# Recommendation tower on one core: ids counted from a partition's first row for two halves, and eight tables read by one-hot columns in the first half in place of seven

## The reference

```
e = jnp.stack([tbl_0[ids[:, 0]], ..., tbl_26[ids[:, 26]]], axis=1)   # 2048 x 27 x 128
dot = jnp.einsum('bnd,bmd->bnm', e, e)                               # pairs i < j are kept: 351
h = jnp.concatenate([z, dense_ctx], axis=1)                          # 367
h = jnp.maximum(h @ W_top1 + b_top1, 0.0)                            # 512
h = jnp.maximum(h @ W_top2 + b_top2, 0.0)                            # 256
y = h @ W_top3
```

## Time and profile before

| | |
|---|---|
| median of 3 runs | 383.13 us (382.71 to 384.81) |
| profiled execution, its own time | 381.17 us |
| its span (first to last instruction) | 379.3 us |
| PE busy | 345.7 us, 91% |
| DVE busy | 294.4 us, 78% |
| POOL busy | 269.3 us, 71% |
| ACT busy | 153.3 us, 40% |
| mean granted TensorE clock | 0.987 of full speed |

### The profile page before, as it was taken

The page is one execution under the profiler, slowest core; times in us unless marked ns, Lnnn a source line. Parts: engine busy times, 40 slices in busy tenths (PEclk is TensorE's granted clock), DMA queues, the critical chain, the costliest instruction groups (busy, mean ns, idle before and its releaser), DMA issues.

```text
span 379.3 us, 9954 instructions
## 1 busy us (share of the span) xinstructions
PE 345.7 (91%) x4035; PEld 322.6 (85%) x4035; DVE 294.4 (78%) x821; ACT 153.3 (40%) x217; POOL 269.3 (71%) x287
## 2 busy tenths in 40 slices
PE   1788868599999999999999999999999999999985
PEld 1677767588999999998999999998999999998874
DVE  4986696898688969798689969798689869793432
ACT  3352644434343453534343453534243453533421
POOL 6777877777777777777777777777777777777400
PEclk9989996999999999999999999999999999999999
DMA  6995225953333333334333333333343343221100
GB/s 184 251 247 136 64 63 137 213 186 96 82 93 85 79 84 82 95 69 95 82 94 85 79 86 81 95 72 91 85 91 85 76 89 83 76 57 50 36 2 1
DMA packets 22988, 36.38 MB, mean 96 GB/s; under 512 B 6224, under 2 KB 17120, under 8 KB 22944
## 3 DMA queue, kind: packets, MB, share of 16 engines
q0 software_dynamic: 8896, 18.24, 20.2%
q1 hardware_dynamic: 14048, 17.52, 18.6%
HBM read 35.73 MB, written 0.01 MB: 94 GB/s over the span
## 4 chain that ended last, share of the span: by engine, by line
PE 75%; POOL 14%; issue 5%; DMA 3%; ACT 2%; DVE 1%; ACTq 0%; DVEq 0%
PE embT_ps L410 35%; PE gram_ps L442 13%; POOL emb L379 12%; PE h_ps L470 11%; PE h_ps L494 7%; PE embT_ps L420 6%; DMA emb<-in_tbl,idx 3%; PE flat_ps L453 2%; POOL flatT L379 2%; ACT embT L634 1%; DVE flat L568 1%; DMA idx<-in_idx_rows 0%; PE h_ps L481 0%; PE flat_ps L481 0%; DVE flat L569 0%
## 5 line engine op out<-in xcount | busy, mean ns | idle before, releaser
L379 POOL DMA_INDIRECT emb<-in_tbl,idx x272 | 261.8, 962 | 83.8 <-issue 80.6
L537 DVE TENSOR_SCALAR one_hot<-ids,row_of 125x256 fp32r<-125x256 int32 x658 | 205.4, 383 | 13.2 <-PE embT_ps L410 10.6
L410 PE MATMUL embT_ps<-one_hot,tbl 125*128 125x256 f32 x1284 | 182.0, 297 | 13.0 <-DVE one_hot L537 11.4
L410 PEld LDWEIGHTS embT_ps<-one_hot,tbl 125*128 125x128 f32 x1284 | 166.7, 196 | 17.9 <-issue 8.9
L634 ACT COPY embT<-embT_ps 128x256 f32<-128x256 f32 x77 | 48.0, 624 | 134.2 <-PE embT_ps L410 129.0
L642 ACT COPY embT<-embT_ps 128x512 f32<-128x512 f32 (+1 forms) x80 | 80.7, 1012 | 11.7 <-PE embT_ps L420 11.7
L568 DVE STREAM_TRANSPOSE flat<-gram_ps 128x864 f32<-128x864 f32 x31 | 33.5, 1082 | 43.7 <-PE gram_ps L442 43.1
L442 PEld LDWEIGHTS gram_ps<-embT 128*59 128x59 f32 x1984 | 56.2, 134 | 9.6 <-ACT embT L634 3.9
L442 PE MATMUL gram_ps<-embT 128*59 128x54 f32 x1984 | 60.2, 217 | 3.8 <-ACT embT L634 2.3
L420 PE MATMUL embT_ps<-ident,emb 128*128 128x128 f32 x272 | 43.8, 276 | 11.6 <-DMA emb<-in_tbl,idx 8.6
L420 PEld LDWEIGHTS embT_ps<-ident,emb 128*128 128x128 f32 x272 | 32.2, 142 | 13.8 <-DMA emb<-in_tbl,idx 11.4
(11 more groups left out here) (47 smaller groups left out, 85.0 us busy)
## 6 DMA issues: line engine op xcount, KB each, us to landing
ids<-in_ids_hot SPq DMA_DIRECT2D x77, 128.0 KB
emb<-in_tbl,idx POOLq DMA_INDIRECT x272, 3.1
embT<-in_tbl SPq DMA_DIRECT2D x5, 448.0 KB
w_sb<-in_tbl SPq DMA_DIRECT2D x3, 560.0 KB
w_sb<-in_W_ring SPq DMA_DIRECT2D x1, 756.0 KB
w_sb<-in_W_top SPq DMA_DIRECT2D x1, 512.0 KB
h1T<-in_tbl SPq DMA_DIRECT2D x1, 448.0 KB
w_sb<-in_tbl SPq DMA_DIRECT2D x1, 448.0 KB
```

What stands on the lines that cost most here:

```text
L379: pool.indirect_dma_start(gathered_row(t, s), None, tables[f][:, :], bass.IndirectOffsetOnAxis(ap=idx[:, t, f:f + 1], axis=0),).then_inc(g ...
L410: mm = pe.matmul(out[:, 0:HN], tbl[0:ROWS, part, AT[o] + chunk, :], one_hot[0:ROWS, k % SLOTS, c, :], start=(chunk == 0 and part == 0), st ...
L537: done = dve.tensor_scalar(one_hot[0:ROWS, k % SLOTS, c, :], of, row_of[0:ROWS, KINDS.index(CH[o]), chunk:chunk + 1], None, ALU.is_equal)
```

## The change

Two things are edited. `READ_IN_HALF[0]` goes from 7 to 8: table number 7 is read by one-hot columns in half 0 as well, and tiles 0 and 1 gather 19 tables each. And for the builds of halves 0 and 1 (`RELATIVE` = 8 + 10 = 18 steps) ACT first turns the ids in their buffer into floats, the number of the partition's first row minus the id; DVE then compares that float with the constant -c for chunk c, in place of an int32 with a column of `row_of`. Builds from half 2 on are as before. In the start SP loads the ids of step 0 ahead of table 0 instead of behind it.

```diff
-READ_IN_HALF = (7, 10, 10, 10, 10, 10, 10, 10)
+READ_IN_HALF = (8, 10, 10, 10, 10, 10, 10, 10)
@@
+    RELATIVE = len(HOT0) + len(hots_of(1))
@@ SP
+            load_ids(0)
             for o in range(SHARED + 1):
                 load_table(o)
-                if o < len(HOT0):
+                if 0 < o < len(HOT0):
                     load_ids(o)
@@ DVE, build(n)
-                dve.wait_ge(ids_loaded[n % IDS], 16 * (n // IDS + 1))
+                if n < RELATIVE:
+                    dve.wait_ge(ids_relative, n + 1)
+                else:
+                    dve.wait_ge(ids_loaded[n % IDS], 16 * (n // IDS + 1))
...
+                        if n < RELATIVE:
+                            done = dve.tensor_scalar(columns, of.bitcast(F32), float(-chunk), None, ALU.is_equal)
+                        else:
+                            done = dve.tensor_scalar(columns, of, row_of[0:ROWS, KINDS.index(CH[o]), chunk:chunk + 1],
+                                                     None, ALU.is_equal)
@@ ACT
+            def relative_ids(n):
+                act.wait_ge(ids_loaded[n % IDS], 16 * (n // IDS + 1))
+                if n == 0:
+                    act.wait_ge(rows_ready, len(KINDS))
+                kind = KINDS.index(CH[HOTS[n][2]])
+                act.activation(ids[0:ROWS, n % IDS, :].bitcast(F32), ids[0:ROWS, n % IDS, :], ACT.Identity,
+                               bias=row_of[0:ROWS, kind, 0:1], scale=-1.0).then_inc(ids_relative, 1)
@@
             AHEAD = 3
+            relative_ids(0)
             for o in range(AHEAD):
                 split_high(o)
+                if o > 0:
+                    relative_ids(o)
@@ in the loop over ORDER, ahead of the copy of a hot step
+                    if n + AHEAD < RELATIVE:
+                        relative_ids(n + AHEAD)
```

More of the change, by code:

```diff
@@ L281, in dlrm_tower @@
         low_ready = sem("low_ready")
+        ids_relative = sem("ids_relative")
         ids_loaded = [sem(f"ids_loaded{b}") for b in range(IDS)]
@@ L536, in build @@
                         chunk = i * GROUP + c
-                        done = dve.tensor_scalar(one_hot[0:ROWS, k % SLOTS, c, :], of,
-                                                 row_of[0:ROWS, KINDS.index(CH[o]), chunk:chunk + 1], None,
-                                                 ALU.is_equal)
+                        columns = one_hot[0:ROWS, k % SLOTS, c, :]
+                        if n < RELATIVE:
[3 more added lines that the diff above has]
+                                                     None, ALU.is_equal)
                     done.then_inc(hot_built, 1)
```

## The result

| | before | after |
|---|---|---|
| median | 383.02 us (380.39 to 384.81, 9 runs) | 386.69 us (386.04 to 389.67, 9 runs) |
| profiled execution | 381.17 | 386.81 |
| span | 379.3 | 385.0 |
| ratio | | 1.0126, 95% interval 1.0091 to 1.0161 |

The change made the kernel slower by 1.3%. I had forecast no change that a measurement can tell (-0.6 us), so the sign was wrong. The number is almost that of my first rival (386.9), but not its mechanism, as the profile and the experiments show.

A forecast was written before the change was run, and what follows sets the result against it. POOL's gathers up to PE's last wait at 81.35 were taken to bind, then fixed PE work. -2.5 (two gathers) + 2.2 (contention) - 0.3 (small losses) = -0.6 us: profiled 380.6, median 382.5, range 379.5 to 387.5.

The forecast's parts named there:

- first rival: Gathers lose the shared pair to whole groups of new builds, 6.6 us; 386.9 us, chance 0.27.
- The step that failed: ACT's wait for ids n+3 ahead of copy n, in half 1: requested when build n-1 is done; taken as 0.
- The cover: PE's 11.0 us of idle time from 38 to 82 us, taken to hide delays there.
- The two gathers: Two fewer gathers, in tiles 0 and 1, ahead of PE's last wait: 2.5 us less on the bounding chain.
- The eighth table's 4.2 us of PE work: Half 0: net 4.2 us more PE work ahead of 39 us, covered by 14.3 us idle; taken 0.
- 0.9 us later: Tile 0 would end 0.9 us later, less a transpose, from the new order of tables between quads; taken 0.
- The new build: DVE builds, halves 0 and 1: 0.17 us each at double rate against 0.314, saving 21 us less 1.7, off the chain.
- the reason I gave against the Trainium skill's rule: Old build's 0.314 us means its operand column or int32 holds it at the single rate, despite the rule.
- The gathers beside new builds: 54 gathers on POOL wait for double-rate builds holding the shared pair: 2.2 us more, between 0 and 6.6.
- 0.3 of small losses: Small gather losses beside old builds, 3 ahead of 82 us, would go: 0.3 us less.
- PE's last wait: Sign of a wrong forecast: before PE's full stretch, this wait is for ACT or one_hot instead of a gather.
- The sum without the failed step: Whole-kernel forecast of -0.6 us, in which the wait for ids counted 0; forecast's chance 0.38.

The follow-up runs named there:

- f1: Kernel after, with the loads of tables 8 and 9 and layer 1's weights two places later in SP's queue, behind ids; 382.66 us, 1.0018 to before.
- f4: f3, with ScalarE waiting for the ids where the conversions stood, converting nothing; 389.98 us, 1.0228 to the kernel before.
- f3: Kernel before with only READ_IN_HALF[0] = 8: eight tables, old builds, no conversions; 380.85 us, 0.9974 to the kernel before.
- f2: Kernel after with READ_IN_HALF[0] back to 7, keeping new builds and conversions; 385.83 us, 1.0102 to the kernel before.
- g1: Kernel after with conversions and new builds for the first 13 steps in place of 18; 381.24 us, 0.9993 to the kernel before.
- g3: f1 with ids kept int32, compared with a constant; one run, 381.02 us, only record lengths read (306 ns on average).
- g4: f1 with float ids compared with an operand column in SBUF; one run, 379.89 us, only record lengths read (385 ns on average).

## Why the prediction was wrong, point by point

- **The step that failed** is the one on ScalarE's wait: "In half 1 the ids for n+3 are asked for when build n-1 is done. Taken: 0." The semaphore was right, the queue was left out. The request for ids n+3 stands in SP's queue behind loads that wait for something else, and twice these are tables 8 and 9, which wait for splits. Before, nobody needed these ids until later: only VectorE waited for them, at its own build 13. The change put the wait three steps earlier, on the engine that also empties PE's banks and starts the splits. In numbers: 0 was taken; the kernel after against f1 says 1.1% of 383, 4 us, and f4 against f3 says 2.5%, some 9 us without the new builds.
- **The cover.** I had 11.0 us of PE's idle time from 38 to 82 us as cover for anything of ScalarE's. It was used: pauses of 9.49 and 8.91 us on ScalarE became 4.22 and 3.41 us on PE, in place of waits for gathers, and the reads behind them ran at half clock, 1.6 us longer each than at full clock (3.78 against 2.14). The kernel before had slow reads as well (3.04 and 3.45 us), so against it the same steps took only about 1.9 us more work, and against f1 about 4.0. That a pause costs clock on top of its own length was not in the sum.
- **The two gathers** (-2.5): right for the gathers. f3 has the 54th gather 2.5 us earlier than the 56th was. How much of it reaches the end is smaller, -1.0 us with an interval from -2.1 to +0.1 (0.9974).
- **The eighth table's 4.2 us of PE work** at no cost: right by f2 and f3. But tile 0 did not end 0.9 us later: tile 1's first quad, at 38.01 before, is at 39.86 in f3, and at 41.40 in the kernel after and 41.41 in f2. So the 3.4 us are there without the table too, with the new start (conversions, new builds, the order of the ids); PE's first read already starts at 10.58 in place of 8.52. f3 and g1 (40.98) show that such a delay was covered.
- **The new build**: I said 0.17 us from start to start if it takes the double rate. It took 0.226 (eight in 1.81 us) against 0.314, so VectorE saved an estimated 13 us (152 x 0.088) and not 21. That it saved any speaks for the reason I gave against the Trainium skill's rule ("VectorE: DVE Perf Modes", section "What auto-detection actually checks"): by that rule the old form had the double rate too, and g3 and g4 disagree; an operand column in SBUF in place of the constant takes it away. That the type doesn't matter agrees with the rule.
- **The gathers beside new builds** (+2.2): there, but about half. Up to the 54th gather, losses of up to 0.25 us each sum to 1.8 us in the kernel after and 1.8 in f1, against 0.6 before and 0.7 in f3: 1.2 us more. The sum took 0.3 of small losses away; they grew. Long ones, beside splits, are 3.0 us before, 2.5 in the kernel after and 4.8 in f1, by where the splits fall.
- **The first rival** gave 386.9 and the measurement is 386.7, but it was to come from gathers. In the kernel after the 54th gather started at 73.17, 2.7 us earlier than the 56th before, when the rival wanted it 4 us later. POOL's last gather was early too (352.57 against 354.70). The right number came from a wrong cause; the place to see that was PE's last wait, and the prediction had named it: "if PE's last wait before its full stretch were for ACT or for one_hot [...] the wait for ids in front of the copies, binds".
- **The sum without the failed step** can be read off f1 and g1, the same kernel without the two waits: -0.6 us was forecast; f1 gives +0.7 (interval -0.6 to +2.0) and g1 -0.3 (-1.4 to +0.8). Both hold the forecast, but neither is clean: f1 moves the load of layer 1's weights as well, and g1 has five steps of old builds more.

## What to carry to other kernels

When a wait for a transfer is moved earlier or to another engine, follow the transfer back through its queue and not only to its semaphore: list what is issued ahead of it, what each of these waits for, and whether one of them waits for work that stands behind the new wait. Idle time of the matmul engine is poorer cover than its length says: behind pauses of 4.22 and 3.41 us the reads ran at half clock. A long VectorE instruction with two SBUF inputs beside a stream of indirect DMAs can be cut into pieces: here the gathers came 3.4 us earlier by it, though how much of that the end gained isn't clear of noise.

## What the runs showed of the hardware that I hadn't expected

A tensor_scalar of 125x256 from SBUF to SBUF takes 0.226 us from start to start with a constant and 0.314 with a [P, 1] column in SBUF as its operand, with int32 ids in the old build and float ids in g4; g3 has 0.226 with a constant and int32. A gather waited for a whole split of 1.49 us (2.09 us in place of 0.94), but took 1.03 beside back-to-back pieces of 0.35 us; so here the two engines took turns by instruction. The traces agree in this with the Trainium skill, "SBUF — State Buffer", section "Who interferes with whom", which says that a VectorE instruction with two SBUF inputs contends with a GpSimd instruction that reads SBUF, and that the shared pair is an exclusive lock.
